# The value matmuls of the third attention layer, given once per unit of four key heads instead of once per step of two

## The reference, cut to what matters

```
q = (query @ Wq).reshape(b, sq, 32, 16)      # query: the normalised x
k = (key @ Wk).reshape(b, sk, 8, 16)         # key and value: ctx_4096
v = (value @ Wv).reshape(b, sk, 8, 16)
k = jnp.repeat(k, 4, axis=1)                 # 4 query heads share a key head
v = jnp.repeat(v, 4, axis=1)
scores = einsum('bhqd,bhkd->bhqk', q, k) * 16 ** -0.5
probs = softmax(scores, axis=-1)
out = einsum('bhqk,bhkd->bhqd', probs, v)    # the value matmuls
return out.reshape(b, sq, 512) @ Wo
```

## Time and profile before

| | |
|---|---|
| median of three runs | 1305.55 us |
| the profiled execution, its own time | 1308.82 us |
| its span, first to last instruction | 1306.5 us |
| mean granted TensorE clock | 0.869 |
| PE busy | 981.9 us, 75% |
| PEld (weight loads) busy | 687.7 us, 53% |
| DVE busy | 786.2 us, 60% |
| ACT busy | 478.4 us, 37% |
| POOL busy | 440.9 us, 34% |

### The profile page before, as it was taken

One profiled execution on the slowest core, in us unless ns is written; L12 is line 12 of the kernel. 1 busy time (PEld: TensorE's weight loads), 2 busy tenths in 40 slices (PEclk: granted clock), 3 DMA queues, 4 the chain that ended last, 5 costly groups with the idle time before them and its releaser, 6 DMA issues. The chain is left out here.

```text
span 1306.5 us, 15618 instructions
## 1 busy us (share of the span) xinstructions
PE 981.9 (75%) x5219; PEld 687.7 (53%) x5219; DVE 786.2 (60%) x1270; ACT 478.4 (37%) x677; POOL 440.9 (34%) x375
## 2 busy tenths in 40 slices
PE   3888885869999999305872339899877467687995
PEld 1666652656666667104761128744463245455774
DVE  4656656677776777465248953467644799533322
ACT  1434332326666666013323133344402355343130
POOL 3333212226666766222221543100010521244424
PEclk9889975979999999757985559899997799788998
DMA  7000012046778665812010031000001100130001
GB/s 268 1 2 1 1 49 86 2 152 218 246 254 297 234 234 194 302 60 97 33 57 0 0 113 65 18 1 1 1 1 64 65 18 1 47 99 24 1 1 65
DMA packets 32270, 110.11 MB, mean 84 GB/s; under 512 B 4480, under 2 KB 4800, under 8 KB 28864
## 3 DMA queue, kind: packets, MB, share of 16 engines
q1 hardware_dynamic: 24672, 84.47, 18.1%
q0 software_dynamic: 7520, 24.65, 5.8%
HBM read 130.07 MB, written 16.78 MB: 112 GB/s over the span
## 5 line engine op out<-in xcount | busy, mean ns | idle before, releaser
L1027 POOL DMA_INDIRECT f_picks<-f_turn_xn,f_target x47 | 113.2, 2408 | 71.3 <-ACT f_turn_xn L967 71.0
L1328 PE MATMUL banks<-f_t_dn,f_z 128*128 128x512 f32 x188 | 88.5, 593 | 0.6 <-issue 0.6
L206 PE MATMUL banks<-ident,a_turn_xn 128*128 128x128 f32 x64 | 16.2, 413 | 84.6 <-DVE a_turn_xn L214 84.6
L103 POOL TENSOR_TENSOR a_ahead_var_eps<-mean_var,eps 128x1 f32<-128x1 f32 x32 | 6.1, 189 | 190.3 <-DVE mean_var L99 190.3
L1162 DVE TENSOR_TENSOR f_gu_lo<-f_t_gu,f_gu_hi 128x2048 fp32r<-128x2048 f32 x24 | 55.0, 2293 | 13.1 <-ACT f_gu_hi L953 11.8
L1021 POOL DMA_INDIRECT f_turn_xn<-f_xn_rows,f_token x47 | 47.8, 1017 | 41.7 <-DVE f_token L1156 17.9
L1162 DVE TENSOR_TENSOR f_xn_lo<-f_t_gu,f_xn_hi 128x2048 fp32r<-128x2048 f32 x23 | 52.7, 2293 | 13.5 <-ACT f_xn_hi L953 13.0
L206 PEld LDWEIGHTS banks<-ident,a_turn_xn 128*128 128x128 f32 x64 | 11.2, 209 | 90.2 <-DVE a_turn_xn L214 90.1
L443 POOL TENSOR_TENSOR a_k<-a_kf,a_k_sel 128x512 fp32r<-128x512 f32 x16 | 20.2, 1262 | 103.1 <-ACT a_k_sel L463 103.1
L2137 ACT ACTIVATE a_e<-banks 128x1024 f32<-128x1024 f32 x32 | 32.8, 1023 | 52.4 <-PE banks L2236 52.3
L480 ACT ACTIVATE a_e<-banks 128x1024 f32<-128x1024 f32 x32 | 32.5, 1015 | 47.4 <-PE banks L654 47.4
(11 more groups left out here) (455 smaller groups left out, 3034.7 us busy)
## 6 DMA issues: line engine op xcount, KB each, us to landing
f_t_gu<-in_f_gu SPq DMA_DIRECT2D x47, 1024.0 KB
f_t_dn<-in_f_dn SPq DMA_DIRECT2D x47, 512.0 KB
f_t_gu<-f_picks SPq DMA_DIRECT2D x6, 1024.0 KB, 8.2
raw<-in_ctx_turned SPq DMA_DIRECT2D x4, 1024.0 KB, 6.1
raw<-in_ctx_rows SPq DMA_DIRECT2D x4, 1024.0 KB, 4.8
f_xn_rows<-f_turn_xn SPq DMA_DIRECT2D x9, 256.0 KB, 2.1
x_res<-in_x SPq DMA_DIRECT2D x8, 256.0 KB, 4.8
a_ctx<-in_ctx SPq DMA_DIRECT2D x2, 1024.0 KB, 7.6
```

Source lines behind the costliest of these rows:

```text
L206: mm = pe.transpose(self.core.psum[:, self.first_bank + b % 2, c * P:(c + 1) * P], self.xn[:, b % self.rows, c * P:(c + 1) * P], self.core ...
L1027: pool.indirect_dma_start(dram["f0_picks_flat"], bass.IndirectOffsetOnAxis(ap=target[:, t:t + 1], axis=0), t_y[:, t % F0_BUFS, :], None).t ...
L1328: mm = pe.matmul(ps[:, TY_BANK + t % 2, :], t_zt[:, t % 2, c, :], t_dn[:, t % F0_BUFS, c, :], start=c == 0, stop=c == F0_IC - 1)
```

## The change

`values` takes a unit instead of a step and gives the matmuls of all four heads. It is called in even steps only, in the place where the second half stood before. It waits for both exponentials of its unit, and its waits for `on_ready` and `ot_lo_ready` are the same as before. `mm` of the last head signals `pv_done`, as before.

```
-                def values(s):
-                    u = s // 2
+                def values(u):
                     b, g = divmod(u, A2_GROUPS)
-                    pe.wait_ge(exp_ready, s + 1)
+                    pe.wait_ge(exp_ready, 2 * u + 2)
                     if u >= 2:
                         pe.wait_ge(on_ready, u - 1)
                     if u % 2 == 1 and b >= 1:
                         pe.wait_ge(ot_lo_ready, b)
-                    for i in range(2 * (s % 2), 2 * (s % 2) + 2):
+                    for i in range(A2_PER_GROUP):
                         mm = pe.matmul(ps[A2_VSLOT * i:A2_VSLOT * (i + 1), O_BANK + u % 2, :],
                                        v[:, b // HB, b % HB, g * A2_PER_GROUP + i, :], e[:, u % 2, i, :],
                                        start=True, stop=True)
-                    if s % 2 == 1:
-                        mm.then_inc(pv_done, 1)
+                    mm.then_inc(pv_done, 1)
...
                     if s < STEPS:
                         keyed(s)
-                    if 1 <= s <= STEPS:
-                        values(s - 1)
+                    if s % 2 == 0 and 2 <= s <= STEPS:
+                        values(s // 2 - 1)
                     if s + 1 < STEPS:
                         turn_max(s + 1)
```

## The result

The changed kernel takes 1315.7 us as the median of 20 runs (1308.32 to 1321.42); the kernel before, run beside it, takes 1306.35 us (1301.06 to 1318.93). The ratio is 1.0066 with a 95% interval of [1.0046, 1.0087], so it is slower by 6.0 to 11.4 us. A second measurement beside later experiments gave 1.0048 [1.0022, 1.0074]. The profiled execution took 1315.15 us with a span of 1312.8 us.

What follows compares the result with a forecast made beforehand. The stage was taken to alternate between DVE's maximum and PE, with PE's granted clock mattering too. Terms: -4.4 saved, 0 in even steps, +10.8 for falls, +6.4 us on 1305.55: 1312.0 us; 8-in-10 range 1301 to 1322 us.

Steps and rivals of the forecast that it cites:

- Odd steps with s % 4 == 1: These and s = 3: transposes start 0.05 us behind the maximum, saving 0.28 us in each of 8 steps, 2.2 us.
- s % 4 == 3: Odd steps where `turned_lo` makes the maximum late: 0 saved, PE gap of 1.66 us before the transposes.
- The end of the loop: s = 31 and 32: the last value group waits only for the last exponential, saving 1.2 us.
- Step 1: s = 1, at the low clock: transposes no longer wait for the value matmuls, saving 1.0 us.
- Even steps: Four heads run beside each other; the group still takes 1.05 us, covered by DVE's maximum: 0 added.
- The rival of two by two: Even steps: four heads run two by two, costing 13.6 us less 4.4, 1314.8 us; chance 0.10.
- Falls: Holes behind `turn_on` in the loop: PE's thin work drops the granted clock in 6 of 7, 10.8 us in all.
- Price of a fall: Loop at the low clock: 0.36 us lost for each us, taken as 1.8 us per fall.
- The rival that the clock holds: No stretch behind `turn_on` is followed by a clock below 1.00; the 4.4 us saving remains, 1301.2 us; chance 0.20.

Runs made afterwards that it cites:

- fill_hole: Changed kernel with two value matmuls given once more in odd steps with s % 4 == 3; 1304.95 us, ratio 0.9974 to the kernel before.
- fill_hole_one: Changed kernel with one added value matmul of 512 columns in odd steps with s % 4 == 3; 1305.38 us, ratio 0.9991 to the kernel before.
- hybrid_odd: Kernel before, with only odd-numbered units giving four heads at once, which empties the hole behind `turn_on`; 1313.86 us, ratio 1.0069.
- hybrid_even: Kernel before, with only even-numbered units giving four heads at once, value matmuls behind `turn_on` kept; 1306.83 us, ratio 1.0011.
- fill_odd: Changed kernel with two value matmuls given once more in every odd step with a `turn_max`; 1303.45 us, ratio 0.9967 to the kernel before.

## Why the prediction was right

The forecast was +6.4 us, 1312.0 us, for the median; the ratio gives +6.0 to +11.4 us. The mechanism held step by step, with these sizes:

- *Odd steps with s % 4 == 1.* The transposes start 0.05 us behind the maximum (888.52 + 1.22 = 889.74, then 889.79), as worked out; fill_hole's batches are 0.29 us shorter for it.
- *s % 4 == 3.* No gain, and a gap of 1.66 us, the figure of the forecast.
- *The end of the loop.* The group starts at 951.24, right behind the exponential's end at 951.18, as worked out.
- *Step 1.* The transposes no longer wait for the value matmuls, but with step 1 emptied the low clock of the start lasted 3.4 us longer, 13.7 us in place of 10.2, which at 0.42 us for each us is 1.4 us. The 1.0 us was counted without that.
- *Even steps.* Eight records take 1.06 us: four heads run side by side. The rival of two by two is out. The Trainium skill (TensorE: Matmul & The Clock Gate, packing small matmuls) gives a speedup of 2.38 for three column strips. No run here has three; four strips took the time of two, and of the single one in fill_hole_one (1.05 us).
- *Falls.* Six were forecast; the two profiles show six and five. The forecast counted seven holes and took six of them, but the loop has six: the step behind the last `turn_on`, s = 31, has no transposes of maxima that could wait. So in one profile every hole had its fall, in the other all but one, and that the count came out is in part luck. Without the start the first profile spent 38.1 - 13.7 = 24.4 us at the low clock in the loop, 0.5 us of it in the fall that begins at the very end.
- *Price of a fall.* Against fill_hole, which has the same groups of four, the loop is 118.8 - 108.8 = 10.0 us longer with 38.1 - 14.3 = 23.8 us more at the low clock: 0.42 us for each us, where 0.36 was taken. The second profile gives (115.9 - 108.8) / (31.8 - 14.3) = 0.41. So a fall costs 10.0 / 6 = 1.7 us, where 1.8 was taken.

In the profiled executions the loop grew by 7.6 us. The output projection behind it grew by 1.5 us, as the low stretch that begins at the loop's end lasted 6.8 us in place of 3.4, which the sum did not have. First the kernel before, then the changed one:

```profile
950.30:953.70 3.40, 3.08 (x7) 0.50 0.00 0
956.00:962.80 6.80, 6.18 (x15) 0.50 0.00 0
```

The forecast of 6.4 us is short by about these two terms, the longer low clock at the start and at the end. The whole profiled execution is only 6.3 us longer, because the first attention layer, the same code in both, took 2.8 us less in the second; that this total lies so close to the forecast is luck.

The rival that the clock holds rested on the wording of the Trainium skill (same page, Why this matters for your kernels), which ties a return to the low clock to long idle gaps. Here gaps of 1.66 us were followed by a fall, six times in one profile, with matmuls on either side. For this loop the trace speaks against reading it as a safe rule.

That the clock is the cause is shown by experiment: filling the hole with work that is thrown away removes the falls and the loss, changing only the units that empty it (hybrid_odd) brings both, and changing as many units elsewhere (hybrid_even) brings neither.

## What to carry to other kernels

Where PE waits in a loop for another engine, look at the granted clock before taking work out of that wait: matmuls that cost nothing there may be what holds the clock. Compacting PE's work saves only what stood in front of the next waiter, and it opens holes elsewhere; keep matmuls in the longest hole of the loop, real ones if there are any. In a loop that already shows falls, a matmul into a bank that is overwritten anyway can pay, as in the first attention layer: 0.9903.

## What the runs showed of the hardware that was not expected

- Two float32 streams of 64 stationary columns each, in the place of four of 32, take the same time (1.08 us for four records at the full clock), but in both profiles some of their low stretches lasted 13.7 us, where those of the changed kernel behind its holes lasted 3.4 us, with one of 6.8 us. The cause is open.
- A fall in the loop's last steps reaches into what follows: the output projection took 25.1 us without a low stretch in it (fill_odd and both hybrids), 26.5 us with one of 3.4 us (the kernel before) and 27.7 to 28.0 us with one of 6.8 us (the changed kernel twice, fill_hole).
